# Reordered ScalarE, VectorE and TensorE work in a fused attention and expert layer, and a routing table made in six pieces instead of two

## The chip, the cores and the metric

The kernel runs on one core of one Trainium2 chip. The metric is the device time of one execution in microseconds (us). Five engines run side by side, each through its own instructions in program order, and wait for one another on semaphores: PE (TensorE, matrix products and transposes), ACT (ScalarE), DVE (VectorE), POOL (GpSimd) and SP (SyncE, which here only issues transfers).

## The reference, cut to what matters

2048 tokens of width 128 go through windowed attention (16 heads of 8, each query sees the 64 keys up to itself), a residual and a layer norm, and then through the two best of 8 experts, again with a residual and a layer norm.

```
x = layernorm(x + attn(x, w_qkv, w_out, b_out))
logits = x @ gate_w + gate_b;  topv, topi = top_k(logits, 2);  probs = softmax(topv)
for e in range(8):
    z = (x @ w1[e] + b1[e]) * (x @ w2[e] + b2[e])
    y = silu(z @ wg[e] + bg[e]) @ w3[e] + b3[e]
    out += (sum of probs where topi == e) * y
x = layernorm(x + out)
```

## The kernel before

**Attention in slots.** The tokens are 16 tiles of 128; two tiles form a unit of 256 whose queries, keys and values are projected together. Each engine has a function `slot(t, s)` that is called once per tile and lists, by hand, what that engine does in that slot for several tiles at different stages; a few slots are written out, slots 4 to 11 are a loop of four bodies. The order in which the calls stand in `slot` is the engine's order of work. A call with `later(t, -2)` works on the tile of two slots ago. Slots with an even number are even slots: they project keys and values; odd slots turn the tokens and project queries.

**One tile's way.** PE makes rough scores against slotted keys (`max_scores`, line 1349, from `k_slots` and `q_quarters`); DVE takes the row maxima (`find_top`, 949) and spreads them (`spread_top`, 959, tile `shift`); PE makes the exact scores less the maxima (`shifted_scores`, 1366 and 1370, from the stacked `q_stack` and `k_stack`), in two halves, a = 0 and a = 1; ACT takes exponentials (`exps`, 810); PE weighs the values (1385) into `o_bank`; ACT copies that bank out (`copy_values`, 821, tile `o_raw`); PE transposes it (`turn_values`, 1395); DVE takes reciprocals of the denominators and divides (`denominators` 973, `divide` 979); PE transposes again (`heads_T`, 1400), ACT copies (`oT`, 816), PE projects (1405). Then DVE and POOL normalise, and route: `x1_T` 1419, gate logits 1426, DVE logits 1017, ranks 1432, places 1043 to 1060, scatter to the DRAM table `routed` by POOL (664).

**A unit's way to the stacks.** In an even slot PE projects the keys of a unit used two slots later (1315). ACT copies their rounded part (788), DVE the rest (`split_keys`, 1008, tile `k_parts`). SP waits for it, stores both to DRAM (418), issues eight loads into `q_stack` (409) and four into `k_stack` (422), then four loads of expert weights. From the same rounded part ACT makes the four `key_slots` (795), needed by `max_scores` at the start of the next slot. In odd slots ACT copies the projected queries (774) and makes four `q_quarters` from them (779), needed only a slot after the next one's start.

**Expert stage.** The tokens are then worked on in 39 tiles of 128 routed rows, again in slots (`tile_slot`), with five stages of different tiles in one slot. Tiles 0 to 16 come from a table made on DVE after 12 of the 16 token tiles (`early_table`), the other 22 from a second table that DVE makes within the first tile slots. `run_end` calls a piece of remaining work after each of the first slots: `pieces` names them. Each step of a table is a `link`: one small DVE instruction, and a wait for its own completion. SP waits for the whole second table ahead of its load for tile 17 (in slot 14), PE and POOL ahead of tile 17.

## Time and profile before

| | |
|---|---|
| median of 3 runs | 317.65 us (317.65 to 318.34) |
| profiled execution: its time, and the span of its trace | 318.13 us, 316.3 us |
| attention, from `heads_T` of slot 4 to that of slot 12: 61.54 to 128.79 us | four units, 67.25 us |
| expert tiles | about 162 to 291 us |
| PE, DVE, ACT, POOL busy, share of the span | 76%, 69%, 48%, 50% |

The profile follows one execution. Busy time counts an engine's own instructions; a row of the timeline ends in square brackets where the engine stood idle ahead of it, with the instruction that released it. A row that ends in x4 stands for four instructions merged from the first start to the last end.

### The profile page before, as it was taken

To read this page: it belongs to the slowest core of one execution; us is meant where nothing else is said; L and a number is where in the kernel's file an instruction comes from. 1 tells how busy PE (TensorE), PEld (TensorE's weight loads), DVE (VectorE), ACT (ScalarE), POOL (GpSimd) and SP (SyncE) were. 2 spreads that over 40 slices of the span, in tenths; PEclk is the share of its full clock that TensorE was granted. 3 is DMA by queue.
4 is the path that set the end of the run, shared out by engine and by line. 5 is a ranking of instruction groups with operands and counts; after the bars stand their busy time and mean duration, and the time that the engine had idled before them with its cause. 6 is when DMAs were issued, how large, how long until landed. Compare 5 with 4: busy or idle time off the path is not lost.

```text
span 316.3 us, 7675 instructions
## 1 busy us (share of the span) xinstructions
PE 241.9 (76%) x1791; PEld 177.1 (56%) x1791; DVE 218.1 (69%) x714; ACT 153.3 (48%) x410; POOL 159.2 (50%) x287
## 2 busy tenths in 40 slices
PE   2485798787878788898588775999999999996000
PEld 1154576565667666687355554767677667664000
DVE  5499645778777878786747577687777777674091
ACT  3554636677666677755325542344443443442043
POOL 6654002556566656667763472333455455546151
PEclk9998959999999999999859999899999999999555
DMA  4662625249685968685521021311111111100522
GB/s 130 182 161 68 172 72 135 68 138 272 188 233 168 253 177 233 183 229 181 214 71 37 9 60 36 100 45 52 51 53 37 38 45 53 39 26 7 181 119 99
DMA packets 33988, 36.50 MB, mean 115 GB/s; under 512 B 4972, under 2 KB 30062, under 8 KB 33824
## 3 DMA queue, kind: packets, MB, share of 16 engines
q1 hardware_dynamic: 30864, 29.69, 32.8%
q0 software_dynamic: 2336, 4.37, 4.0%
q10 hardware_dynamic: 752, 2.03, 1.9%
q8 instruction: 14, 0.23, 0.3%
q14 instruction: 22, 0.18, 0.2%
HBM read 25.48 MB, written 11.05 MB: 115 GB/s over the span
## 4 chain that ended last, share of the span: by engine, by line
PE 60%; DVE 11%; ACT 11%; issue 9%; DMA 4%; DVEq 1%; POOL 1%; SPq 1%; ACTq 0%; POOLq 0%
PE bank L1551 10%; PE bank L1523 10%; PE bank L1514 6%; PE bank L1366 5%; PE bank L1370 4%; PE bank L1385 3%; PE bank L1349 3%; PE bank L1395 3%; ACT k_slots L795 3%; PE bank L1546 3%; ACT q_quarters L779 2%; PE bank L1539 2%; PE bank L1347 2%; ACT probs L810 2%; PE bank L1315 2%
## 5 line engine op out<-in xcount | busy, mean ns | idle before, releaser
L713 POOL DMA_INDIRECT expert_out<-probs,tile_x x39 | 40.4, 1035 | 57.7 <-DVE probs L1245 56.2
L810 ACT ACTIVATE probs<-bank 128x512 f32<-128x512 f32 x64 | 35.0, 595 | 39.7 <-PE bank L1370 39.7
L664 POOL DMA_INDIRECT routed<-rows,place x32 | 33.8, 1057 | 21.4 <-issue 16.5
L1523 PE MATMUL bank<-w_gate,x_all 128*128 x156 | 41.2, 388 | 0.4 <-DVE v_aug L1236 0.4
L1551 PE MATMUL bank<-w_up,x_unit 128*128 x78 | 41.4, 613 | 0.0
L949 DVE TENSOR_REDUCE top<-bank 128x4 f32<-128x384 f32 x64 | 33.5, 549 | 8.7 <-PE bank L1349 7.9
L1250 DVE TENSOR_TENSOR w_rows<-bank,b_up 128x512 f32<-128x512 f32 x39 | 26.9, 689 | 17.3 <-PE bank L1551 17.1
L1514 PEld LDWEIGHTS bank<-w_down,xT 128*128 128x128 f32 x156 | 20.8, 193 | 31.9 <-issue 31.9
L959 DVE TENSOR_TENSOR shift<-top,delta_block 64x256 fp32r<-64x256 f32 x64 | 31.0, 485 | 8.5 <-PE bank L1370 6.9
L883 ACT COPY x_unit<-bank 128x128 f32<-128x128 f32 x39 | 10.3, 265 | 53.8 <-PE bank L1531 53.8
L1514 PE MATMUL bank<-w_down,xT 128*128 x156 | 27.4, 299 | 8.2 <-DVE y_in L1231 5.8
L1366 PE MATMUL bank<-q_stack,k_stack 128*128 128x256 f32 x128 | 29.3, 311 | 1.2 <-issue 1.2
L1523 PEld LDWEIGHTS bank<-w_gate,x_all 128*128 128x128 f32 x156 | 27.2, 195 | 2.7 <-issue 0.4
L1370 PE MATMUL bank<-shift,shift_w 128*128 128x256 f32 x128 | 26.5, 290 | 0.0
L1349 PE MATMUL bank<-k_slots,q_quarters 128*128 128x384 f32 x64 | 25.9, 464 | 0.0
L1366 PEld LDWEIGHTS bank<-q_stack,k_stack 128*128 128x128 f32 x128 | 21.1, 202 | 1.6 <-issue 1.6
L1385 PE MATMUL bank<-probs,v_aug 128*32 128x128 f32 x512 | 21.9, 292 | 0.0
L1347 PE MATMUL bank<-mask_q,rep_b 128*128 128x256 bf16 x60 | 17.9, 299 | 4.6 <-ACT k_slots L795 2.1
L1254 DVE TENSOR_TENSOR x_all<-w_rows 128x256 f32<-128x256 f32 x39 | 19.8, 507 | 1.3
L898 ACT ACTIVATE v_aug<-v_aug 128x256 f32<-128x256 f32 x39 | 16.5, 422 | 8.7 <-DVE v_aug L1236 8.2
L1370 PEld LDWEIGHTS bank<-shift,shift_w 128*128 128x128 f32 x128 | 20.7, 198 | 0.0
L628 POOL TENSOR_SCALAR inv_std<-mean_var 128x1 f32<-128x1 f32 x16 | 4.6, 286 | 31.7 <-DVE mean_var L998 31.5
(177 smaller groups left out, 539.6 us busy)
## 6 DMA issues: line engine op xcount, KB each, us to landing
k_stack<-k_scratch SPq DMA_DIRECT2D x28, 160.0 KB, 3.2
q_stack<-q_scratch SPq DMA_DIRECT2D x62, 64.0 KB, 2.3
tile_x<-routed SPq DMA_DIRECT2D x39, 65.0 KB, 1.8
k_scratch<-k_parts SPq DMA_DIRECT2D x7, 320.0 KB, 2.4
q_scratch<-q_parts SPq DMA_DIRECT2D x8, 256.0 KB, 2.4
w_up<-in_L_ffn_w_dram SPq DMA_DIRECT2D x16, 128.0 KB
w_gate<-in_L_ffn_wg_dram SPq DMA_DIRECT2D x8, 256.0 KB
b_up<-in_L_ffn_b_dram SPq DMA_DIRECT2D x2, 1024.0 KB
```

What stands on the lines that cost most here:

```text
L664: eng.indirect_dma_start(routed, bass.IndirectOffsetOnAxis(ap=place[i][:, k:k + 1], axis=0), rows[i][:, k, :], None, bounds_check=SPARE + ...
L713: eng.indirect_dma_start(expert_out, bass.IndirectOffsetOnAxis(ap=tile_x[i][:, P:P + 1].bitcast(I32), axis=0), y[i][:, :], None, bounds_ch ...
L810: eng.activation(probs[t[1] % 2][a][:, 512 * h:512 * h + 512], t_bank[h][:, :], ACT.Exp).then_inc(probs_ready, 1)
L949: eng.tensor_reduce(top[a][:, 4 * h:4 * h + 4], s_bank[h][:, 0:4 * BLOCK_KEYS].rearrange("p (s k) -> p s k", s=4), AX_X, ALU.max).then_inc ...
L959: eng.tensor_tensor(shift[a][half][r, :, :].rearrange("p s (b q) -> p b s q", b=2), top[a][r, :].rearrange("p (b s) -> p b s", b=2).unsque ...
L1349: eng.matmul(scores, q_quarters[i][:, 2 * w + h, :, :].rearrange("p g q -> p (g q)"), k_slots[i][:, :, at:at + BLOCK_KEYS], start=False, s ...
L1366: eng.matmul(t_bank[h][:, 256 * l:256 * l + 256], k_stack[i][:, grp, QT * w:QT * w + P], q_stack[i][:, grp, :, QT * w:QT * w + QT], start= ...
L1370: ins = eng.matmul(t_bank[h][:, 256 * l:256 * l + 256], shift_w[:, h, l, first, :], shift[a][h][:, :, :], start=False, stop=(l == 1), skip ...
L1385: ins = eng.matmul(o_bank[32 * j:32 * j + 32, o:o + P], v_aug[i][:, w, j, 2 * HD * pair:2 * HD * pair + 32], probs[t[1] % 2][a][:, c:c + P])
L1514: ins = eng.matmul(down_bank[:, 0:P], actT[m[1] % 2][:, c, :], w_down[:, bass.ds(e[4], 1), c, :].rearrange("p o n -> p (o n)"), start=(c = ...
L1523: ins = eng.matmul(gate_bank[:, 0:F], zT[m[1] % 2][:, c, :], w_gate[:, bass.ds(e[2], 1), c, :].rearrange("p o n -> p (o n)"), start=(c == ...
L1551: eng.matmul(up_bank[:, :], tile_xT[n[1] % 2][:, :], of_expert(w_up, e[0])).then_inc(up_made, 1)
```

## The change: what it does

ACT, even slots: `key_slots` stands ahead of the second exponentials, and `copy_values` ahead of `values`. ACT, odd slots: `queries` is split, and `copy_values` goes between the copy of the queries and the four query blocks. PE: `turn_values` moves behind the first `shifted_scores`. DVE: the first `spread_top` moves ahead of `denominators` and `divide`. The second table's two pieces (after tile slots 6 and 7) become six (after slots 6 to 11); the 14 links are the same. SP pads the ends of the expert regions after slot 8, as before.

```diff
-            pieces = {0: "values", 1: "project", 2: "ranks", 3: "x1", 4: "logits", 5: "places", 6: "totals", 7: "table",
-                      8: "rows"}
+            pieces = {0: "values", 1: "project", 2: "ranks", 3: "x1", 4: "logits", 5: "places", 6: "totals", 7: "need",
+                      8: "ends", 9: "passed", 10: "jumps", 11: "table"}
...
                 eng.activation(q_parts[:, 0, :], unit_bank[:, 0:UNIT], ACT.Copy, scale=SCALE).then_inc(q_hi, 1)
+
+            def query_blocks(u):
+                i = u[1] % 2
                 wait(eng, q_hi, ucount(u, 1, 1))
...
-                if has(s, 0, STEPS - 1):
-                    exps(t, 1)
                 if s == -2:
...
-                if t[1] % 2 == 0 and has(s, 0, STEPS - 2):
-                    values(unit_at(t, 0))
+                if has(s, 0, STEPS - 1):
+                    exps(t, 1)
                 if odd:
                     queries(unit_at(t, 3))
                 if has(s, 1, STEPS):
                     copy_values(later(t, -1))
+                if odd:
+                    query_blocks(unit_at(t, 3))
+                if t[1] % 2 == 0 and has(s, 0, STEPS - 2):
+                    values(unit_at(t, 0))
...
+                if find:
+                    spread_top(top_t, 0, 0)
+                    spread_top(top_t, 0, 1)
                 if adds:
                     denominators(res_t)
                     divide(res_t)
-                if find:
-                    spread_top(top_t, 0, 0)
-                    spread_top(top_t, 0, 1)
...
                 elif name == "totals":
+                    rest_totals()
+                elif name == "need":
                     rest_needed()
+                elif name == "ends":
+                    rest_ends()
+                elif name == "passed":
+                    passed_of(REST, table_chain)
+                elif name == "jumps":
+                    jumps_of(REST, rest_row0[:, :], table_chain)
                 elif name == "table":
                     rest_table()
...
+                if has(s, 0, STEPS - 1):
+                    shifted_scores(t, 0)
                 if has(s, 2, STEPS + 1):
                     turn_values(later(t, -2))
-                if has(s, 0, STEPS - 1):
-                    shifted_scores(t, 0)
```

The new functions hold the old links: `rest_totals` the total and the two instructions of the padding rows, `rest_needed` three links, `rest_ends` three, `passed_of` two, `jumps_of` three, and `table_of`, called by `rest_table`, two.

ACT's order in even slot 12, before (`probs` are the exponentials, `k_parts` the rounded keys, `oT` the turned heads, `v_aug` the values, `o_raw` the weighted values):

```order
L810 ACTIVATE probs<-bank 128x512 x2
L827 COPY x1T<-bank 128x128
L788 CAST k_parts<-bank 128x320
L816 COPY oT<-bank 128x128
L810 ACTIVATE probs<-bank 128x512 x2
L795 ACTIVATE k_slots<-k_parts,slot_col 128x320 x4
L802 COPY v_aug<-bank 128x16x2x16
L821 COPY o_raw<-bank 128x2x4x64
L831 ACTIVATE gap<-gap 128x1
```

The same slot in the changed kernel, where lines from 774 on stand three further down:

```order
L813 ACTIVATE probs<-bank 128x512 x2
L830 COPY x1T<-bank 128x128
L791 CAST k_parts<-bank 128x320
L819 COPY oT<-bank 128x128
L798 ACTIVATE k_slots<-k_parts,slot_col 128x320 x4
L813 ACTIVATE probs<-bank 128x512 x2
L824 COPY o_raw<-bank 128x2x4x64
L805 COPY v_aug<-bank 128x16x2x16
L834 ACTIVATE gap<-gap 128x1
```

The key slots passed the second exponentials, and `o_raw` passed `v_aug`. The end of ACT's odd slot 3, before:

```order
L816 COPY oT<-bank 128x128
L810 ACTIVATE probs<-bank 128x512 x2
L774 ACTIVATE q_parts<-bank 128x256
L779 ACTIVATE q_quarters<-q_parts,quarter_col 128x8x32 x4
L821 COPY o_raw<-bank 128x2x4x64
L831 ACTIVATE gap<-gap 128x1
```

The same place in the changed kernel:

```order
L819 COPY oT<-bank 128x128
L813 ACTIVATE probs<-bank 128x512 x2
L774 ACTIVATE q_parts<-bank 128x256
L824 COPY o_raw<-bank 128x2x4x64
L782 ACTIVATE q_quarters<-q_parts,quarter_col 128x8x32 x4
L834 ACTIVATE gap<-gap 128x1
```

The copy of the weighted values now stands ahead of the four query blocks. DVE in even slot 12, before, from the second row maximum on (`shift` is the spread maxima, `o_den` and `o_norm` the reciprocals and the division, `logits` the gate's):

```order
L949 TENSOR_REDUCE top<-bank 128x4
L41 REGISTER_ALU
L973 RECIPROCAL o_den<-bank 128x16
L979 TENSOR_TENSOR o_norm<-bank,o_den 128x128
L959 TENSOR_TENSOR shift<-top,delta_block 64x2x4x32 x2
L1008 TENSOR_TENSOR k_parts<-bank,k_parts 128x320
L1017 TENSOR_TENSOR logits<-bank,gate_bias 128x8
```

And in the changed kernel:

```order
L954 TENSOR_REDUCE top<-bank 128x4
L964 TENSOR_TENSOR shift<-top,delta_block 64x2x4x32 x2
L41 REGISTER_ALU
L978 RECIPROCAL o_den<-bank 128x16
L984 TENSOR_TENSOR o_norm<-bank,o_den 128x128
L1013 TENSOR_TENSOR k_parts<-bank,k_parts 128x320
L1022 TENSOR_TENSOR logits<-bank,gate_bias 128x8
```

The two spreads no longer stand between the division and the logits; in odd slots, which split no keys, nothing stands there.

## Rows read from the trace of the kernel before

**Rows 1.** Busy by stretch: length, PE, PEld, DVE, ACT, POOL, clock, DMA share, GB/s

```profile
61.54:128.79 67.25, 55.15 (x604) 43.83 (x601) 52.16 (x200) 46.05 (x117) 42.13 (x89) 1.00 0.72 204
```

**Rows 2.** Timeline of PE: start us, us, operation, idle before and releaser

```profile
40.31 0.77 PE L1366 MATMUL bank<-q_stack,k_stack 128*128 128x256 f32 x2 [1.22 <-issue]
...
49.78 0.32 PE L1341 MATMUL bank<-mask_q,rep_b 128*128 128x384 bf16 x1 [1.08 <-issue]
...
58.81 0.63 PE L1395 MATMUL bank<-ident,o_raw 128*128 128x128 f32 x4 [1.68 <-ACT o_raw L821]
...
103.66 0.33 PE L1400 MATMUL bank<-ident,o_norm 128*128 128x128 f32 x1
...
109.43 0.63 PE L1395 MATMUL bank<-ident,o_raw 128*128 128x128 f32 x4 [1.80 <-ACT o_raw L821]
...
117.07 0.33 PE L1341 MATMUL bank<-mask_q,rep_b 128*128 128x384 bf16 x1 [1.08 <-ACT k_slots L795]
...
147.21 0.66 PE L1395 MATMUL bank<-ident,o_raw 128*128 128x128 f32 x4 [0.57 <-ACT o_raw L821]
```

**Rows 3.** Timeline of ACT, end of an odd slot and of the next even one

```profile
106.98 1.71 ACT L779 ACTIVATE q_quarters<-q_parts,quarter_col 128x256 fp32r<-128x256 f32 x4
108.59 0.56 ACT L821 COPY o_raw<-bank 128x512 f32<-128x512 f32 x1
...
113.96 1.09 ACT L810 ACTIVATE probs<-bank 128x512 f32<-128x512 f32 x2 [1.16 <-PE bank L1370]
114.93 1.91 ACT L795 ACTIVATE k_slots<-k_parts,slot_col 128x320 fp32r<-128x320 f32 x4
```

**Rows 4.** Timeline of DVE, an odd slot's logits to the next slot's key split

```profile
104.15 0.17 DVE L1017 TENSOR_TENSOR logits<-bank,gate_bias 128x8 f32<-128x8 f32 x1 [0.41 <-PE bank L1426]
...
107.35 0.42 DVE L1002 SCALAR_TENSOR_TENSOR q_parts<-bank,q_parts 128x256 fp32r<-128x256 f32 x1
...
108.39 1.02 DVE L949 TENSOR_REDUCE top<-bank 128x4 f32<-128x384 f32 x2
110.10 0.26 DVE L973 RECIPROCAL o_den<-bank 128x16 f32<-128x16 f32 x1 [0.69 <-PE bank L1395]
110.46 0.29 DVE L979 TENSOR_TENSOR o_norm<-bank,o_den 128x128 f32<-128x128 f32 x1
111.05 0.87 DVE L959 TENSOR_TENSOR shift<-top,delta_block 64x256 fp32r<-64x256 f32 x2 [0.30 <-PE bank L1370]
112.18 0.49 DVE L1008 TENSOR_TENSOR k_parts<-bank,k_parts 128x320 fp32r<-128x320 f32 x1 [0.26 <-ACT k_parts L788]
```

**Rows 5.** Timeline of SP's issues, the same unit's key stacks

```profile
118.50 1.97 SPq L422 DMA_DIRECT2D k_stack<-k_scratch  x4
```

**Rows 6.** The page's transfers: count, KB each, median us from issue to landing

```profile
k_stack<-k_scratch SPq DMA_DIRECT2D x28, 160.0 KB, 3.2
```

**Rows 7.** Timeline of DVE, tile slots 6 to 10: each begins with y_in

```profile
185.33 0.29 DVE L1231 TENSOR_TENSOR y_in<-bank,b_down 128x128 f32<-128x128 f32 x1 [0.65 <-issue]
...
190.32 0.29 DVE L1231 TENSOR_TENSOR y_in<-bank,b_down 128x128 f32<-128x128 f32 x1 [1.15 <-issue]
...
192.45 0.15 DVE L1122 SCALAR_TENSOR_TENSOR jump<-need,taken_step 1x8 f32<-1x8 f32 x1
...
194.48 0.17 DVE L1083 TENSOR_SCALAR tile_row<-probs 1x22 int32<-1x22 f32 x1
195.64 0.29 DVE L1231 TENSOR_TENSOR y_in<-bank,b_down 128x128 f32<-128x128 f32 x1 [0.99 <-DVE tile_row L1083]
...
198.41 0.29 DVE L1231 TENSOR_TENSOR y_in<-bank,b_down 128x128 f32<-128x128 f32 x1 [0.56 <-issue]
...
202.71 0.29 DVE L1231 TENSOR_TENSOR y_in<-bank,b_down 128x128 f32<-128x128 f32 x1 [0.59 <-issue]
```

**Rows 8.** Busy by stretch, columns as in group 1, 10 us of tile slots

```profile
190.00:200.00 10.00, 6.88 (x29) 5.37 (x30) 7.24 (x24) 2.25 (x8) 2.59 (x3) 0.83 0.21 61
```

More of the change, by code:

```diff
@@ L541, in piece @@
             def piece(name):
-                if name == "rows":
+                if name == "ends":
                     pad_ends()
@@ L1072, in ends_of, with passed_of @@
                 link(eng.tensor_reduce(ends[:, :], ends_2[:, :, :], AX_X, ALU.add), chain)
-            def tiles_of(first, n, row0, chain):
+            def passed_of(n, chain):
                 link(eng.tensor_tensor(passed[:, 0:n, :], ends[:, :].unsqueeze(1).to_broadcast([1, n, E]),
@@ L1078, in tiles_of, with jumps_of @@
                 link(eng.tensor_reduce(table_f[:, 0, 0:n], passed[:, 0:n, :], AX_X, ALU.add), chain)
+            def jumps_of(n, row0, chain):
                 link(eng.tensor_tensor(jumps[:, 0:n, :], passed[:, 0:n, :], jump[:, :].unsqueeze(1).to_broadcast([1, n, E]), ALU.mult), chain)
@@ L1081, in tiles_of, with table_of @@
                 link(eng.tensor_tensor(table_f[:, 1, 0:n], table_f[:, 1, 0:n], row0, ALU.add), chain)
+            def table_of(first, n, chain):
                 link(eng.tensor_scalar(tile_expert[:, 4 + first:4 + first + n], table_f[:, 0, 0:n], float(E - 1), None, ALU.min), chain)
@@ L1096, in early_table @@
                 link(eng.tensor_scalar(jump[:, :], need[:, :], -float(P), float(REGION), ALU.mult, ALU.add), early_chain)
-                tiles_of(0, FULL, tile_row0[:, 0:FULL], early_chain)
+                passed_of(FULL, early_chain)
+                jumps_of(FULL, tile_row0[:, 0:FULL], early_chain)
+                table_of(0, FULL, early_chain)
                 link(eng.tensor_scalar(taken_upto[:, 1:E + 1], ends[:, :], float(FULL), None, ALU.min), early_chain)
@@ L1104, in early_table, with rest_totals @@
                 assert links[0] == EARLY_LINKS
-            def rest_needed():
+            def rest_totals():
                 links[0] = 0
@@ L1113, in rest_needed @@
                 eng.tensor_copy(pad_row[:, :], pad_f[:, :]).then_inc(pad_chain, 1)
+            def rest_needed():
                 link(eng.tensor_tensor(need_16[:, :, :], total[:, :].unsqueeze(2).to_broadcast([1, E, 16]),
@@ L1117, in rest_needed, with rest_ends, rest_table @@
                 link(eng.tensor_tensor(need[:, :], need[:, :], taken[:, 0:E], ALU.subtract), table_chain)
+            def rest_ends():
                 ends_of(need, table_chain)
-            def rest_table():
                 link(eng.scalar_tensor_tensor(out=jump[:, :], in0=need[:, :], scalar=-float(P), in1=taken_step[:, :],
                                               op0=ALU.mult, op1=ALU.add), table_chain)
-                tiles_of(FULL, REST, rest_row0[:, :], table_chain)
+            def rest_table():
+                table_of(FULL, REST, table_chain)
                 assert links[0] == LATE_LINKS
```

## The prediction

> **What bounds the kernel now.** I read the busy time by stretch first, to see which stage is worth what, then the timelines of PE, ACT and DVE in the attention loop beside the chain of waits, then DVE's in the first expert slots. Over four units of attention PE is busy 55.15 of 67.25 us [rows 1]: a unit takes 16.81 us and PE works 13.79 of them, so 3.0 us are PE's idle time, at a granted clock of 1.00, which is 2.4 GHz. PE's timeline names the idle time [rows 2]: in an even slot it waits 1.80 us for the copy of the weighted values, and at the start of the next odd slot 1.08 us for the key slots. ACT's timeline says why [rows 3]. The copy ran at 108.59, behind 1.71 us of query blocks that no one needs before the next even slot; the key slots ran at 114.93, behind two exponentials of 1.09 us that PE needs only a slot later. The same two waits stand in all four units, so this stage is bound by the order of work on ACT, with PE close behind it.
>
> In the expert stage PE and DVE are about even. One slot is special: a tile slot without a piece runs from 195.64 to 198.41, that is 2.77 us, on DVE alone, while the two slots with a table piece take 4.99 (185.33 to 190.32) and 5.32 (to 195.64), and one more takes 4.30 (198.41 to 202.71) [rows 7], when the granted clock had fallen (0.83 on average, a mixture of 2.4 and 1.2 GHz) [rows 8].
>
> **ACT and PE, the units.** Both waits go if the copy comes 1.71 us earlier and the key slots 1.09 us earlier. With nothing in their place a unit would take PE's 13.8 us. I do not expect that, because two other loops are close.
>
> *DVE.* I walk DVE's order with rows [rows 4]. From an odd slot's logits at 104.15 to the next slot's first row maximum at 108.39 it takes 4.24 us without a pause, of which 0.42 is the query split that an even slot lacks: 3.82 there. Then come two maxima (1.02), the two spreads (0.87), the reciprocal with its gap (0.36) and the division (0.29), 2.5 us together. Before, the spreads stood behind the division, and worked while PE made the next thing that DVE needs. Now nothing does in an odd slot: DVE waits while PE transposes the divided heads and multiplies by the gate, 0.49 us from 103.66 [rows 2] to 104.15, and some 0.06 more for the semaphore (an estimate): a hole of 0.55. In an even slot the key split (0.49) fits in it. Odd: 4.24 + 2.5 + 0.55 = 7.3; even: 3.82 + 2.5 + 0.55 = 6.9; a unit 14.2, or 14.7 if ACT's rounding of the keys comes so late that the split follows the hole.
>
> *The stacks.* A unit's keys go through DRAM, and the loads must have landed when `shifted_scores` of the slot after the next begins. From the end of the key split (112.67) [rows 4] to the last issue, some 1.5 us into the four that start at 118.50 [rows 5], and 3.2 us to landing [rows 6], it is 10.5 us; nearly all of it is SP issuing one transfer after another. Before it, from the start of the turn at 109.43 to the split's end, 3.24 us hold one turn and the first `shifted_scores`; the new order swaps the two, so it is 3.24 us from the start of `shifted_scores`. 3.24 + 10.5 = 13.75 us, and 14.35 where the query blocks, now last in ACT's slot, push the first exponentials and the rounding of the keys back by some 0.6 (an estimate from the 1.71 us of rows 3, less what PE's maxima and first scores cover). So this loop, hidden today, becomes a bound as close as DVE.
>
> I take 14.6 us for a unit, near the upper ends, since both loops must be met in each slot. Four units: 67.25 - 58.4 = **8.85 us** won; bounds 13.8 (12.1 won) and 15.8 (4.0 won, below).
>
> *Second exponentials late.* They are now behind the key slots. In the trace they start 4.53 us after the turn (113.96 from 109.43) [rows 2, 3]; in the new order the key slots can start at about 3.24, end at 5.15, and the exponentials at 6.24. The next `shifted_scores` that needs their bank starts a slot later: 115.99, where PE ran out of work (117.07 less 1.08), plus two maxima of about 0.3 each, is 7.2 us after 109.43. The cover is 0.9 us; what goes beyond it is paid on PE. I take nothing. The values' copy behind the weighted values' is wanted only a slot later: nothing.
>
> **First units.** In slot 2 PE already waits for a stack, 1.22 us to 40.31 [rows 2]. There the turn was done in the waiting time; now it stands behind it, which costs its 0.63. The waits of 1.08 at 49.78 and 1.68 at 58.81 go [rows 2], and I take off one DVE hole of 0.55: 1.08 + 1.68 - 0.63 - 0.55 = **1.6 us** won; 1.0 to 2.1.
>
> **Last slots.** From slot 12 on there are no new units, DVE's slots lose the query split but have the hole, and the stacks of the last unit come as late as before: nothing. The wait of 0.57 at 147.21 [rows 2] goes, as `turn_values` now comes after 1 us of scores: **0.55 us** won.
>
> **The table.** DVE has no free time in these slots (2.77 us of its own), so its links cost full time wherever they stand; what six pieces can change is the ends. The second piece's links run from 192.45 to 194.65, 2.2 us, but its slot is 2.55 longer than 2.77 [rows 7]: 0.35 are lost as DVE waits for the last link before it reads the experts' numbers, where else that read runs beside the last product. Five of the six pieces end in such a wait, against two: 3 x 0.35 = 1.05 more. Against that, slots 9 and 10 cost 4.30 - 2.77 = 1.53 for the clock, which fell after PE had stood still for 2 us twice; with about 1 us six times I expect it to stay. Won: 1.53 - 1.05, about **0.5 us**, bounds -1 (the clock falls all the same) and +1.6.
>
> The Trainium skill, "VectorE: DVE Perf Modes", section "The DRAIN you can't avoid", states that a semaphore after each Vector instruction cost nothing against one after the last (13.88 us both ways). By that the cut would be free, and this part would give 1.5 instead of 0.5. The rows speak against it here, as what waits is the read behind the link, not a Vector instruction. No page is needed for the sum.
>
> **Sum.** 8.85 + 1.6 + 0.55 + 0.5 = 11.5 us. The profiled execution took 318.13 us (a span of 316.3 and 1.8 around it), which gives 306.6. It lay 0.5 above the median of 317.65, so the median would be 306.1; I take **306.5**, since each loop above has little air.
>
> **The rivals.**
> - *PE alone bounds* (13.8 us a unit): the holes of DVE fall where PE is busy anyway. For it: DVE was busy 52.16 us of 67.25 [rows 1], 13.0 a unit. Against it: its order is strict and the hole is a loop through PE. 67.25 - 55.2 = 12.1 in place of 8.85, and 0.5 more in the first units: 302.7.
> - *The stacks bound harder.* The same bytes come in less time: a DMA share of 0.72 [rows 1] becomes 0.72 x 16.81 / 14.6 = 0.83. If landing and issue stretch by 1.5 us, a unit takes 15.8, and 4.0 us are won in place of 8.85: 311.4. For it: in slot 2 the wait is there already. "DMA: Bandwidth & Descriptors" in the Trainium skill, section "Latency and other measured facts", gives HBM access as 0.2 us on average and 2 us at high load, which would do just this; no row here shows k_stack at a higher share.
> - *The cut is free* (each piece ends as cheaply as a product): 1 us less, 305.5. For it only that the ends of the two old pieces are two cases.
> - *Slower.* If the stacks are late in every unit, the turn, the division and all behind it, which used to run in that wait as in slot 2, now start after it, 0.63 each time. It decides from a landing of about 3.2 + 2.5 = 5.7 us on, where 14.35 becomes 16.85; at 6.5 a unit takes 17.6, and four cost 3.2 more than now: about 319.
> - *No effect*: the copies go earlier, and some other wait of the same size follows, 316 to 318.
>
> **How the numbers follow.** The forecast 0.45, PE alone 0.13, the free cut 0.10, the stacks harder 0.22, no effect 0.04, slower 0.06. About 0.3% (1 us) can be told from no change here. Faster then holds all but the last two, 0.90; same 0.04; slower 0.06. For 8 in 10 the range reaches to PE alone (302.7) below, and just beyond the stacks' case (311.4) above, which leaves out half of each with the last two: 302.0 to 312.0.
>
> **What would show it.** Right: in the profile after, PE's waits for `o_raw` in even slots and for `k_slots` in odd ones are gone, a unit takes 14 to 15 us, DVE is idle about half a microsecond ahead of its logits in odd slots, PE waits for the division at `heads_T`, and now and then at the first `shifted_scores` of an even slot for nothing that an engine released, as at 40.31. In the tile slots 6 to 11 each lasts 3.2 to 4.1 us, and none after them 4.3. Wrong: a unit of 15.5 us or more with PE waiting at 1366 (the stacks); waits at 1366 for exponentials (ACT's new order too late); a granted clock under 1.00 in the loop; or four tile slots from the first piece on that are together no shorter than the 17.4 us from 185.33 to 202.71.

## The result, and the profile after

The changed kernel takes 312.28 us (median of 4 runs, 311.62 to 313.58) against 318.0 us before (4 runs, 317.65 to 320.23): a ratio of 0.9848, 95% interval 0.9808 to 0.9888. That is 5.7 us faster where 11.5 were forecast, and just outside the range. The profiled execution took 311.95 us, with a span of 310.2 (316.3 before). The same kernel's times differ between chips and between runs by more than these first runs show (before: 310.68 to 323.55 in one set below), so each experiment stands against runs of before on its own chip, disturbed runs are left out of the ratios, and lengths read in the traces carry the argument.

First the busy time by stretch, columns as in [rows 1]: the same four units, then 50 us of tile slots.

```profile
59.66:121.43 61.77, 54.78 (x603) 43.87 (x601) 52.40 (x201) 46.69 (x117) 43.00 (x88) 1.00 0.77 220
160.00:210.00 50.00, 41.06 (x210) 27.80 (x208) 34.77 (x115) 20.70 (x58) 19.62 (x28) 1.00 0.16 46
```

Four units take 61.77 us in place of 67.25, so 15.44 each where 14.6 were forecast. PE's work is the same; its idle time is 7.0 us instead of 12.1. PE's timeline of the changed kernel says which waits these are:

```profile
40.61 0.76 PE L1393 MATMUL bank<-q_stack,k_stack 128*128 128x256 f32 x2 [5.47 <-issue]
...
56.81 0.38 PE L1393 MATMUL bank<-q_stack,k_stack 128*128 128x256 f32 x1 [1.19 <-DMA k_stack<-k_scratch]
...
67.05 0.33 PE L1427 MATMUL bank<-ident,o_norm 128*128 128x128 f32 x1 [0.54 <-DVE o_norm L984]
...
72.38 0.47 PE L1393 MATMUL bank<-q_stack,k_stack 128*128 128x256 f32 x2 [1.37 <-issue]
...
88.57 0.50 PE L1393 MATMUL bank<-q_stack,k_stack 128*128 128x256 f32 x2 [1.71 <-DMA k_stack<-k_scratch]
...
103.41 0.47 PE L1393 MATMUL bank<-q_stack,k_stack 128*128 128x256 f32 x2 [0.62 <-issue]
...
113.60 0.33 PE L1427 MATMUL bank<-ident,o_norm 128*128 128x128 f32 x1 [0.52 <-DVE o_norm L984]
...
121.43 0.33 PE L1427 MATMUL bank<-ident,o_norm 128*128 128x128 f32 x1 [0.77 <-DVE o_norm L984]
```

The two waits of [rows 2], for `o_raw` and for `k_slots`, are gone from the units. In their place stand a wait at the first `shifted_scores` (line 1393 now) of even slots, for the key stacks, and one of half a microsecond for the division in each odd slot (and 0.77 in the one even slot that waits for no stack). Both were named in the prediction as loops close behind. What it had wrong is how close.

**The stacks' chain.** SyncE's issues of one unit in the changed kernel:

```profile
76.33 0.42 SPq L418 DMA_DIRECT2D k_scratch<-k_parts  x1
77.05 5.18 SPq L409 DMA_DIRECT2D q_stack<-q_scratch  x8
82.28 1.97 SPq L422 DMA_DIRECT2D k_stack<-k_scratch  x4
...
92.30 0.38 SPq L418 DMA_DIRECT2D k_scratch<-k_parts  x1
```

I read three stretches, from one awaited `shifted_scores` to the next: to the keys' issue to DRAM, from there to the end of the last stack's issue, and from there to PE's start. From 56.81 on they are 3.58 + 8.62 + 3.37 = 15.57 us, from 72.38 on 3.95 + 7.92 + 4.32 = 16.19, from 88.57 on 3.73 + 7.82 + 3.29 = 14.84. The forecast, in the same parts, was 3.24 to 3.84, 7.80 (112.67 to 120.47) and 2.7. Where the trace has the landings, in the first and the third of these units, the last key stack landed at 72.29 and 103.32, and PE began 0.09 us later each time.

**VectorE's loop.** The unit from slot 10 to slot 12 had no wait for a stack; VectorE's timeline there:

```profile
106.77 0.17 DVE L1022 TENSOR_TENSOR logits<-bank,gate_bias 128x8 f32<-128x8 f32 x1
...
110.86 1.02 DVE L954 TENSOR_REDUCE top<-bank 128x4 f32<-128x384 f32 x2
...
113.26 0.29 DVE L984 TENSOR_TENSOR o_norm<-bank,o_den 128x128 f32<-128x128 f32 x1
114.09 0.17 DVE L1022 TENSOR_TENSOR logits<-bank,gate_bias 128x8 f32<-128x8 f32 x1 [0.55 <-PE bank L1453]
...
118.69 1.02 DVE L954 TENSOR_REDUCE top<-bank 128x4 f32<-128x384 f32 x2
...
121.92 0.17 DVE L1022 TENSOR_TENSOR logits<-bank,gate_bias 128x8 f32<-128x8 f32 x1 [0.15 <-PE bank L1453]
```

The hole of 0.55 us is there, as forecast. But from logits to logits it is 7.32 and 7.83 us, a unit of 15.15, not 14.2 to 14.7. The stretch to the next row maximum takes 4.09 and 4.60 (forecast 3.82 and 4.24), the rest 3.23 each time (3.05).

**Where the 6.1 us of the span came from.** `heads_T` of slot 4 is 1.88 us earlier (59.66 against 61.54), the units give 5.48, the last slots 0.45. Then 0.92 is lost up to the first tile slots (`y_in` of slot 6 at 178.44 against 185.33, 6.89 earlier), 0.42 in the slots with the table, and 0.37 after them. Two of these parts hold a share of PE's clock. From `heads_T` of slot 2 to that of slot 3, before and after:

```profile
44.37:53.13 8.76, 7.57 (x78) 6.17 (x74) 4.92 (x14) 5.38 (x14) 2.06 (x5) 0.90 0.53 151
```

```profile
44.70:51.63 6.93, 6.62 (x78) 5.59 (x74) 5.33 (x14) 5.88 (x14) 1.96 (x5) 1.00 0.43 118
```

Of the 1.83 us that this slot gives, 0.95 is PE's own work done at a higher granted clock. From the last `heads_T` but one to the last, beside the first tiles, it is the other way round, before and after:

```profile
158.45:167.05 8.60, 7.64 (x38) 4.62 (x39) 3.70 (x18) 2.18 (x8) 5.46 (x13) 0.59 0.30 72
```

```profile
150.64:160.15 9.51, 8.37 (x37) 4.98 (x38) 3.70 (x18) 2.33 (x8) 6.30 (x13) 0.52 0.42 116
```

Here 0.91 is lost, and PE's own work takes 0.73 longer, at a lower granted clock.

**The table.** VectorE's timeline, `y_in` of tile slots 6 to 12:

```profile
178.44 0.29 DVE L1258 TENSOR_TENSOR y_in<-bank,b_down 128x128 f32<-128x128 f32 x1 [0.64 <-issue]
181.94 0.29 DVE L1258 TENSOR_TENSOR y_in<-bank,b_down 128x128 f32<-128x128 f32 x1 [0.84 <-issue]
185.91 0.29 DVE L1258 TENSOR_TENSOR y_in<-bank,b_down 128x128 f32<-128x128 f32 x1 [1.05 <-issue]
189.67 0.29 DVE L1258 TENSOR_TENSOR y_in<-bank,b_down 128x128 f32<-128x128 f32 x1 [0.99 <-DVE jump L1138]
193.48 0.29 DVE L1258 TENSOR_TENSOR y_in<-bank,b_down 128x128 f32<-128x128 f32 x1 [0.99 <-DVE probs L1083]
197.49 0.29 DVE L1258 TENSOR_TENSOR y_in<-bank,b_down 128x128 f32<-128x128 f32 x1 [0.99 <-DVE probs L1089]
202.06 0.29 DVE L1258 TENSOR_TENSOR y_in<-bank,b_down 128x128 f32<-128x128 f32 x1 [0.99 <-DVE tile_row L1094]
```

and SyncE's issues beside them, with the wait on PE:

```profile
189.61 5.37 SPq L515 DMA_DIRECT2D routed<-pad  x8
195.75 1.48 SPq L530 DMA_DIRECT2D tile_x<-routed  x2
```

```profile
197.86 0.33 PE L1558 MATMUL bank<-ident,tile_x 128*128 128x128 f32 x1 [2.24 <-DMA tile_x<-routed]
```

The clock stays at 1.00 from 160 to 210 us, as forecast (0.83 before, [rows 8]). But all six pieces end in a wait of 0.84 to 1.05 us, where the two slots without a piece in [rows 7] have 0.56 and 0.59. And ahead of slot 11's work a tile's load stands behind eight pads, 5.4 us of SyncE, and PE waits 2.24 us for it. Slots 6 to 12 take 26.38 us in place of 25.96.

### The profile page after: what moved, and what is told of

Same layout as the page of the kernel before. It is cut to its first block, busy times and chain, and to the rows that moved or that the text cites. A ratio compares the mean times of both kernels' runs of the same rounds, so it can differ in the third digit from the quotient of the medians.

```text
span 310.2 us, 7675 instructions
## 1 busy us (share of the span) xinstructions
PE 237.9 (77%) x1791; PEld 174.1 (56%) x1791; DVE 217.2 (70%) x714; ACT 154.1 (50%) x410; POOL 161.0 (52%) x287
## 4 chain that ended last, share of the span: by engine, by line
PE 47%; DVE 14%; SPq 12%; issue 12%; DMA 8%; POOL 3%; ACT 2%; DVEq 0%; ACTq 0%; POOLq 0%
PE bank L1578 9%; PE bank L1550 8%; PE bank L1541 6%; SPq L409 5%; PE bank L1393 3%; DMA k_stack<-k_scratch 3%; PE bank L1573 2%; PE bank L1397 2%; PE bank L1566 2%; PE bank L1412 2%; DMA expert_out<-probs,tile_x 2%; DVE top L954 2%; SPq L422 2%; DVE shift L964 2%; DMA w_up<-expert_out 2%
## 5 line engine op out<-in xcount | busy, mean ns | idle before, releaser
L1550 PE MATMUL bank<-w_gate,x_all 128*128 x156 | 40.4, 382 | 0.5 <-DVE v_aug L1263 0.5
L1277 DVE TENSOR_TENSOR w_rows<-bank,b_up 128x512 f32<-128x512 f32 x39 | 26.8, 688 | 18.5 <-PE bank L1578 18.3
L964 DVE TENSOR_TENSOR shift<-top,delta_block 64x256 fp32r<-64x256 f32 x64 | 30.1, 471 | 11.9 <-PE bank L1397 9.5
L1393 PE MATMUL bank<-q_stack,k_stack 128*128 128x256 f32 x128 | 28.4, 305 | 10.9 <-issue 7.4
L1376 PE MATMUL bank<-k_slots,q_quarters 128*128 128x384 f32 x64 | 25.0, 449 | 0.0
L1412 PE MATMUL bank<-probs,v_aug 128*32 128x128 f32 x512 | 21.1, 283 | 0.0
L628 POOL TENSOR_SCALAR inv_std<-mean_var 128x1 f32<-128x1 f32 x16 | 5.4, 338 | 27.9 <-DVE mean_var L1003 27.2
```

The lines of the kernel that those rows point to most:

```text
L964: eng.tensor_tensor(shift[a][half][r, :, :].rearrange("p s (b q) -> p b s q", b=2), top[a][r, :].rearrange("p (b s) -> p b s", b=2).unsque ...
L1277: eng.tensor_tensor(up[:, :, :].rearrange("p a n -> p (a n)"), up_bank[:, :], of_expert(b_up, e[0]), ALU.add).then_inc(up_ready, 1)
L1393: eng.matmul(t_bank[h][:, 256 * l:256 * l + 256], k_stack[i][:, grp, QT * w:QT * w + P], q_stack[i][:, grp, :, QT * w:QT * w + QT], start= ...
L1412: ins = eng.matmul(o_bank[32 * j:32 * j + 32, o:o + P], v_aug[i][:, w, j, 2 * HD * pair:2 * HD * pair + 32], probs[t[1] % 2][a][:, c:c + P])
L1550: ins = eng.matmul(gate_bank[:, 0:F], zT[m[1] % 2][:, c, :], w_gate[:, bass.ds(e[2], 1), c, :].rearrange("p o n -> p (o n)"), start=(c == ...
```

## The experiments

Lengths of units are from `heads_T` to `heads_T` of even slots. A unit is called clean where PE waits for no stack in it.

**First set: parts undone.** e1_paired loads the expert weights for two experts at a time:

```
-                if s is None:
+                if s is None and t[1] % 2 == 0:
-                        eng.dma_start(w_up[:, bass.ds(e, 1), c, :], ...
+                        eng.dma_start(w_up[:, bass.ds(e, 2), c, :], ...
```

> The changed kernel with the expert weights of two experts in one transfer, issued in the even slots alone: the same bytes, but 4 weight issues a unit on SyncE in place of 8. A unit takes 15.44 us in the changed kernel. Issue theory (SyncE's time to issue transfers one after the other, some 0.5 us each, fills the loop of the stacks): the stacks' last issue comes about 2 us earlier in the unit, PE's waits of 0.6 to 1.7 us at the first shifted_scores of even slots go, a unit takes 14.5 to 14.7, the time is 308 to 309 us. Traffic theory (the same bytes in less time make each transfer land later): the bytes are the same, so the unit stays at 15.3 to 15.5 and the time at 311.5 to 312.5. VectorE theory (its order with the spreads ahead of the division is the bound): the waits at shifted_scores go, but PE waits as long elsewhere, for o_norm or sparse: unit 15.2 or more, time above 311.

Measured: 313.27 us in its profiled execution, 313.27 to 321.62 in four runs, with before at 310.68 to 323.55 beside it, so the time says nothing. PE's waits for the stacks are 1.0 to 3.1 us: longer, not gone. SyncE's issues show that the edit did something else as well:

```profile
100.94 0.38 SPq L458 DMA_DIRECT2D q_scratch<-q_parts  x1
105.05 0.37 SPq L418 DMA_DIRECT2D k_scratch<-k_parts  x1
107.08 1.20 SPq L409 DMA_DIRECT2D q_stack<-q_scratch  x2
```

The queries' transfer to DRAM now stands behind four weight transfers of twice the size, and the query stacks, which wait for it, begin 6.1 us after it and 2.0 behind the keys (0.7 in the changed kernel). So this run doesn't tell the theories apart.

e2_old_dve puts the spreads back behind the division, e3_two_pieces the table back into two pieces, e4_act_only both, and the turn back ahead of the scores:

```
-                if find:
-                    spread_top(top_t, 0, 0)
-                    spread_top(top_t, 0, 1)
                 if adds:
                     denominators(res_t)
                     divide(res_t)
+                if find:
+                    spread_top(top_t, 0, 0)
+                    spread_top(top_t, 0, 1)
```

> The changed kernel with the two spreads behind the division again, as before. VectorE theory (the hole of 0.55 us that this left in each slot bounds the loop): a unit gets up to 1 us shorter, 14.4 to 14.9, and PE's waits of 0.5 us for o_norm in odd slots go: 308 to 310 us. Issue and traffic theories: the waits for o_norm go, the waits for the stacks get longer by as much, unit 15.3 to 15.6, 311.5 to 312.5 us.

> The changed kernel with the second table in two pieces as before, and the pads issued after the second of them; the attention part is untouched. Table slots 6 to 13 take 26.4 us in the changed kernel against 26.0 before. Theory that six ends cost more than they give: 25.5 to 26.0, 311 to 312 us, so 0.4 to 0.9 less than the changed kernel, with the granted clock falling again behind the second piece. Theory of the prediction (two pieces cost 0.5 more through the clock): 312.5 to 313.

> Only the part on ScalarE (key slots ahead of the second exponentials, copies of values ahead of the query blocks); values turned ahead of the scores, spreads behind the division, and the table in two pieces as before. Issue and traffic theories: PE's two waits of 1.80 and 1.08 us go here too, and the stacks bound the unit as in the changed kernel, or come earlier by one turn (0.63 us) less: unit 15.0 to 15.9, 311 to 314 us. If the other edits of the loop carry the gain (the turn behind the scores above all): unit 16 or more, 314.5 us or more. If VectorE's and PE's edits cost time: unit 14.6 to 15.0, 308 to 310 us.

Measured: e2 314.54 us in its profiled execution, with PE's waits for `o_norm` down to one of 0.15 in the units, and waits of 1.4 to 2.7 us for the stacks in three of them; the fourth is clean and takes 14.41. e3: ratio 1.012 (0.994 to 1.030), so the time tells nothing; its table slots take 26.08 us and the clock falls behind the second piece (0.76 over slot 9). Three of its units are clean: two take 14.88 and 15.13, and one 15.76, with a wait of 1.14 us for the division. e4: 0.992 (0.982 to 1.002), 309.11 us when profiled, and its clean unit takes 14.09. By time this set can't place ScalarE's part alone against the whole change. What it shows is that undoing VectorE's part alone mostly turned its wait into a longer one for the stacks (62.73 us for e2's four units against 61.77), and that a unit without such a wait is then shorter (14.41 against 15.15).

**Second set: the same start for all.** In the traces of before and after, VectorE stands still early on. In the changed kernel it is the spread at 23.55:

```profile
23.55 4.13 DVE L964 TENSOR_TENSOR shift<-top,delta_block 64x256 fp32r<-64x256 f32 x2 [0.69 <-PE bank L1397]
27.71 0.49 DVE L1013 TENSOR_TENSOR k_parts<-bank,k_parts 128x320 fp32r<-128x320 f32 x1
```

and on GpSimd at that time:

```profile
22.38 4.57 POOL L677 TENSOR_TENSOR x_all<-x_all,bo 128x2048 f32<-128x2048 f32 x1
```

Two spreads, 0.87 us elsewhere, take 4.13: the first ends at 27.23, 0.28 us behind the end of GpSimd's add at 26.95 (27.44 and 27.16 in the trace of before). Behind them stands the key split, and the second unit's stacks are late by it. The Trainium skill, "SBUF — State Buffer", section "SBUF: two separate sides", says that a VectorE instruction with two SBUF inputs and a GpSimd one that reads SBUF take a shared pair of ports in turns, whole instructions at a time; the trace agrees (4.57 us for the add, 4.13 for the spreads). Four kernels let the add wait for that split; the first is the kernel before, the second, third and fourth are the whole change, ScalarE's part, and ScalarE's part with the stacks in two halves:

```
                 if s == 1:
                     eng.wait_ge(loaded, 16 * 4)
+                    eng.wait_ge(k_lo, 2)
```

```
-                    if s != -2:
-                        wait(eng, k_hi, ucount(u, 1, 1))
-                        wait(eng, k_lo, ucount(u, 1, 1))
-                        store_keys(eng, i).then_inc(k_out, 16)
...
                     for part in range(8):
+                        if s != -2 and part == 4:
+                            wait(eng, k_hi, ucount(u, 1, 1))
+                            wait(eng, k_lo, ucount(u, 1, 1))
+                            store_keys(eng, i).then_inc(k_out, 16)
```

> The kernel before, with one wait more: GpSimd's add of the bias to all tokens (4.56 us, at 22.60 in the trace of before) waits for the second key split on VectorE. In the trace of before two spreads on VectorE, 0.87 us elsewhere, took 5.11 us from 22.78, until that add was over, and the key split, and with it the second unit's stacks, came behind them, at 27.92. In the first of the runs above, where the split stood 0.2 us ahead of the add, it ran at 23.51. Theory that this one add holds VectorE: the split is at about 23.8, PE's wait at slot 2 ends some 4 us earlier, 313.5 to 314.5 us. Rival, the add holds a later instruction as long and the stacks are as late: 317 to 318.

> The changed kernel with that same wait on GpSimd; with the run of before with the wait it shows what the change is worth when the start is the same in both. Theory that the start is apart from the loop: 307.5 to 309 us, 5.5 to 6.5 less than before with the wait; units of 15.0 to 15.6 us. Rival, the gain of the start is lost in the loop to later stacks: 311 or more.

> ScalarE's part of the change alone, with the same wait on GpSimd. Theory that PE's and VectorE's moves cost time (the hole of 0.55 us ahead of the logits in each slot, and the turn that no longer fills the wait for the stacks): units without a wait for the stacks take 14.1 us, as the last of them did in the run of ScalarE's part alone, with it 15.0 to 15.6; 303.5 to 305.5 us, some 3 less than the whole change with the wait. Rival, that those moves are worth nothing either way: within 1 us of the whole change with the wait.

> As the kernel above, with four of the eight query stacks issued ahead of the keys' transfer to DRAM instead of behind it. Chain theory (what is late is the time from the key split through SyncE's issues to the landing): from the keys' issue to the end of the last stack's issue it is 5.2 to 5.8 us instead of 7.6, PE's waits at the first shifted_scores of even slots fall by about 2 us, most to nothing; a unit takes 14.0 to 14.5 us, 301 to 303 us. SyncE theory (the queue is full whatever its order, 14.4 us of issues a unit): waits of 0.3 to 0.8 stay, unit 14.5 to 14.8. Traffic theory (stacks land later under load): waits stay near 1 us, unit 15 or more, 304 to 305 us.

Measured, before being 316.96 us on that chip: e7 312.69 (ratio 0.989, 0.978 to 1.000), e8 306.21 (0.968, 0.958 to 0.978), e9 307.58 (0.965, 0.948 to 0.982), e10 303.14 (0.958, 0.947 to 0.968). The start is worth 4.3 us without the change by the medians, with an interval that reaches 1.000; in e7's trace `heads_T` of slot 4 stands at 55.42 in place of 61.54, and the four units take 67.17 as before. The add then holds a later spread as long (26.21 to 30.17 in e7), but no stack hangs on that one. From the same start the change is worth 6.5 us (2.1%, where the first comparison gave 1.5). e9 against e8 is open by time (302.73 to 309.38); its four units take 61.93 us against 63.55, with a wait for a late stack in every one. e10's time from the keys' issue to the end of the last stack's issue is down to 5.05 us, and two of its units still wait for stacks, 1.28 and 1.59 us.

**Third set: the weights out of the loop.** What delays the stacks: the weights' traffic, or the chain itself? In e11 (the whole change), e12 (ScalarE's part) and e13 (the whole change with the spreads put back), all with the later add and each run once, the loop loads no weights; the last four slots do:

```
-                if s is None:
-                    e = t[0] * 4 + (t[1] - 4)
...
+                    to, w = ((w_up[:, :, 0, :], w1), ...)[s - STEPS + 4]
+                    eng.dma_start(to ..., w ...).then_inc(experts_loaded, 16)
```

> The changed kernel with the later add on GpSimd, and with the expert weights (5 MB, 8 issues a unit) taken out of the loop: they are loaded whole, in one transfer a slot, in the last four slots behind the biases. The end of the kernel then waits for them and its time says nothing; what counts are the units from slot 4 to slot 12. Traffic theory (the stacks land 3.3 to 4.3 us behind their last issue because the weights share the way): landing back under 3 us, PE's waits for the stacks gone, and the unit at what VectorE's order leaves, 14.8 to 15.2 us, as in the units without such a wait so far. Chain theory (SyncE's 7.8 us of issues from keys to last stack): waits of 0.5 us or more stay, unit 14.8 to 15.4 with them.

> ScalarE's part alone, with the later add and with the weights out of the loop in the same way. Traffic theory: no waits for the stacks, and the unit at 14.0 to 14.2 us, all of it PE's work: 0.8 to 1.0 us a unit less than the whole change in the run above, which is then what PE's and VectorE's moves cost. Rival, those moves cost nothing: the same unit in both, within 0.2 us.

> The changed kernel with the later add and the weights out of the loop, and the spreads behind the division again: only the turn behind the scores is left of PE's and VectorE's moves. If the hole that the moved spreads left is the bound: PE's waits for o_norm go and the unit is 14.0 to 14.3 us, as with ScalarE's part alone. If the later turn is what costs: 14.7 or more, with PE waiting for something behind the turn.

Busy by stretch of e11's four units, columns as above, and the two waits on its PE:

```profile
56.25:117.77 61.52, 55.05 (x604) 43.91 (x602) 52.27 (x201) 46.70 (x117) 42.85 (x88) 1.00 0.50 140
```

```profile
69.14 0.36 PE L1389 MATMUL bank<-q_stack,k_stack 128*128 128x256 f32 x1 [1.55 <-issue]
...
84.53 0.50 PE L1389 MATMUL bank<-q_stack,k_stack 128*128 128x256 f32 x2 [0.92 <-DMA k_stack<-k_scratch]
```

```profile
72.48 0.36 SPq L418 DMA_DIRECT2D k_scratch<-k_parts  x1
73.14 5.07 SPq L409 DMA_DIRECT2D q_stack<-q_scratch  x8
78.25 1.97 SPq L422 DMA_DIRECT2D k_stack<-k_scratch  x4
```

The DMA share falls from 0.77 to 0.50, and the four units take 61.52 us instead of 61.77. From the end of the last stack's issue (80.22) to PE's start it is 4.31 us, as in the changed kernel (4.32), and in the unit before, to 69.14, 3.39 against 3.37. So the traffic theory falls, as far as it means the weights of this loop, and with it the reason that the prediction's rival gave. Eight fewer issues a unit change the chain little too: 3.34 + 7.74 + 4.31 = 15.39. e11's clean units take 14.87 and 15.16 us, e12's 14.42 and 14.36, and e13 waits 0.8 to 2.5 us for a stack in all four units. VectorE's and PE's moves together cost 0.5 to 0.8 us a clean unit, and without VectorE's the stacks bind.

> ScalarE's part alone with the later add, four query stacks ahead of the keys, and the expert weights two experts at a time, so that SyncE issues 4 transfers less in each unit. The run without the pairing still waited for the stacks in two units, where SyncE had got round to the keys late. If SyncE's full queue was the reason: at most one such wait, units of 14.0 to 14.6, 300 to 302 us. If landing under load is: the same waits, 302 to 304 us.

e14 took 313.81 us (ratio 0.979, 0.965 to 0.993), slower than e10 against its own before, with waits of 2.5 to 3.1 us for the stacks in three of its four units. Its query stacks wait for a transfer behind doubled weights as in e1. Its trace has the landing: the queries' transfer, issued at 98.11, landed at 104.68, and the query stacks' issues began at 104.70; in the kernel before such a transfer lands 2.4 us after its issue (median). So the pairing lengthened the loop in both orders that were tried.

**Fourth set: each loop shortened.** e15 is e8 with the stacks in two halves, e16 the same with the spreads behind the division, e17 with the turn ahead of the scores too, e18 is e8 again.

> The changed kernel with the later add and four of the eight query stacks issued ahead of the keys; PE's and VectorE's moves stay. If the chain of the stacks and VectorE's order are two loops of nearly the same length: PE's waits at the first shifted_scores go in most units, the waits of 0.5 us for o_norm stay in every slot, the unit is 14.9 to 15.2 us, and the time is some 1 to 2 us under the changed kernel with the later add in the last of these runs. If the stacks alone bound it: 14.1 to 14.5, 3 us or more.

> As the run above, and the spreads behind the division again; the turn stays behind the scores. Two-loops theory: both limits are away, unit 14.1 to 14.6 where no stack is late, 301 to 304 us. If the later turn costs as much as the hole did: 14.8 or more, no faster than the run above.

> As the run above, and the turn ahead of the scores again: ScalarE's part, the table in six pieces, the later add and the stacks in two halves. Against the same with the table in two pieces (303.14 us, in another set of runs) it shows whether the six pieces are worth anything: 0.5 us more or less at most by the table slots so far, so 302 to 304 us. Late stacks still to be seen in one or two units.

> The changed kernel with the later add once more, as what the three runs above stand against: 305 to 308 us, waits of 0.5 to 2 us for the stacks in two or three of the four units.

Measured, before being 319.81 us there: e15 305.25 (ratio 0.954, 0.946 to 0.963), e16 305.65 (0.949, 0.940 to 0.958), e17 305.35 (0.957, 0.948 to 0.966), e18 308.0 (0.963, 0.956 to 0.970). Two clean units of e15, and 4 us around its one late stack:

```profile
85.25:115.62 30.37, 27.89 (x305) 22.27 (x302) 25.79 (x101) 23.00 (x58) 20.00 (x43) 0.98 0.80 216
...
81.00:85.00 4.00, 3.67 (x31) 2.65 (x31) 2.13 (x6) 1.78 (x4) 2.00 (x4) 0.72 0.91 274
```

the waits in e15's PE timeline,

```profile
81.33 0.38 PE L1394 MATMUL bank<-q_stack,k_stack 128*128 128x256 f32 x1 [2.01 <-DMA k_stack<-k_scratch]
...
107.79 0.33 PE L1428 MATMUL bank<-ident,o_norm 128*128 128x128 f32 x1 [0.53 <-DVE o_norm L985]
```

and two units of e16 (the second with one wait of 0.50 us for a stack), with the same `heads_T` row without its wait:

```profile
85.05:113.53 28.48, 27.45 (x304) 21.94 (x300) 25.21 (x100) 23.24 (x58) 18.92 (x43) 1.00 0.83 222
```

```profile
106.25 0.33 PE L1428 MATMUL bank<-ident,o_norm 128*128 128x128 f32 x1
```

15.19 us a unit with the spreads moved, 14.24 with them put back, the turn being in its new place in both: the hole costs 0.95 us a unit once the stacks are out of the way, and the later turn at most 0.2 (14.20 for e16's first clean unit here, 14.01 and 14.02 for those of e10 and e19, where the turn is ahead). e15 and e16 still differ in nothing by time, as late stacks here and there outweigh it (waits of 1.9 to 2.8 us; behind the one above PE runs at a granted clock of 0.72). e15's 2.75 us against e18 came mostly ahead of slot 4, whose `heads_T` is 2.81 earlier. e17 against e10 (0.957 and 0.958 of before) shows no worth in the six pieces; its table slots take 27.01 us, e10's 25.81.

**Last set.**

> ScalarE's part alone, with the table in two pieces, GpSimd's later add and four query stacks ahead of the keys, beside the whole change on the same chip. By the two-loops theory and the start: 302 to 305 us, 6 to 10 less than the whole change and 13 to 15 less than before.

> The whole change once more, on the chip of the run above: 311 to 314 us; PE's wait for the stacks at slot 2 ends at about 40.5 us if GpSimd's add holds VectorE there again, and at 36 to 37 if it doesn't.

e19, which is e10 again, took 303.8 us (303.29 to 305.0; ratio 0.959, 0.954 to 0.965), the whole change on that chip 310.5 (306.75 to 313.71; 0.978, 0.969 to 0.987), before 318.31. e20 is the change without an edit, and its start went the other way:

```profile
23.41 0.87 DVE L964 TENSOR_TENSOR shift<-top,delta_block 64x256 fp32r<-64x256 f32 x2 [1.03 <-PE bank L1397]
24.41 0.49 DVE L1013 TENSOR_TENSOR k_parts<-bank,k_parts 128x320 fp32r<-128x320 f32 x1
24.82 1.01 DVE L954 TENSOR_REDUCE top<-bank 128x4 f32<-128x384 f32 x2
25.93 3.57 DVE L964 TENSOR_TENSOR shift<-top,delta_block 64x256 fp32r<-64x256 f32 x2
```

```profile
24.18 4.60 POOL L677 TENSOR_TENSOR x_all<-x_all,bo 128x2048 f32<-128x2048 f32 x1
```

```profile
36.02 0.47 PE L1393 MATMUL bank<-q_stack,k_stack 128*128 128x256 f32 x2 [2.28 <-issue]
```

GpSimd's add began 1.8 us later than in the first trace; by then the spreads were all but done, the split was not held, and PE's wait at slot 2 ended at 36.02 instead of 40.61; this execution took 308.87 us. So the same kernel has two starts, 4.6 us apart at slot 2, and which one it gets is decided by a race of VectorE with GpSimd. Not all of it reached the end: e20's four units take 63.61 us in place of 61.77, with a wait of 2.19 us for a stack in the first.

## Why the prediction was wrong

The mechanism was right, and sizes of its terms were off, the units' above all. Step by step:

**The waits removed.** Right: PE's waits for `o_raw` and `k_slots` are gone from all four units. Right too that the second exponentials, though later, cost nothing there: none of the waits that PE's timeline shows in the four units is put down to them.

**"I take 14.6 us for a unit, near the upper ends."** This is the step that failed: the term "units" is 5.48 us, not 8.85. Both loops that were meant to bound the unit were taken too short. VectorE's is 14.9 to 15.2 us in clean units of the change, e3, e8, e11, e15 and e20 (with one of 15.76 in e3 and one of 16.12 in e20, where PE waits 1.14 and 1.28 us for the division; why there is open), not 14.2 to 14.7: I walked it on the trace of before, with pieces of an order that no longer holds, and its two slots came out 0.4 and 0.5 us longer. The stacks' chain is 14.84 to 16.19, not 13.75 to 14.35. To the keys it is 3.58 to 3.95 us, the upper end of the forecast or 0.1 beyond it; the issues take up to 0.8 more; and the landing, the largest part, 0.6 to 1.6 more: I took the page's median of one transfer (3.2 us from its issue), but PE waits for the last of twelve, and began 3.3 to 4.3 us after the end of the last issue, where my sum had 2.7. With VectorE's 15.15 alone, the four units would have given 6.65; late stacks took the other 1.2.

**The rival "the stacks bound harder"** came nearest in its number (15.8 us a unit, 311.4), and its reason was wrong: with the DMA share at 0.50 in place of 0.77 the stacks were as late (e11). Of the higher latency at high load that the Trainium skill gives ("DMA: Bandwidth & Descriptors", section "Latency and other measured facts"), and that I weighed for it, no run here shows anything.

**First units, 1.6.** 1.88 came, close by luck: 0.95 of it is the higher granted clock between slots 2 and 3, which the sum did not have, and a wait of 1.19 us for a stack at 56.81, which it did not have either, stands against it. The wait at slot 2 is 5.47 us (1.22 before) and ends at 40.61 as before at 40.31: what the change won ahead of it was lost there, since that stack hangs on GpSimd's add, which the prediction had not seen.

**Last slots, 0.55.** 0.45, but as a net. The wait at 147.21 went, and so did one of 0.94 at 133.57, where the rough scores begin, which I had not counted; waits of 0.78 and 0.80 for the division (128.73 and 135.71) took it back.

**The table, +0.5.** -0.42. The clock stayed up, worth the 1.53 that were forecast (for slot 9; slot 10 took 2.76 before and lost nothing), but the pieces cost 2.0 us more and not 1.05, of which some 0.7 is slot 11 (4.57 us, from 197.49, against 3.5 to 4.0 for the others), where PE waited for a load behind the pads. Two pieces measure 25.6 to 26.8 us over these slots in eight traces, six pieces 26.1 to 27.7 in nine. The reading that the cut is free is refuted.

**Not forecast:** 0.9 us from the last attention slots to the first tiles. Some 0.3 is the first tile's load: PE takes up that tile 7.51 us earlier than before, and its step ahead 7.82. The other 0.6 comes right behind it, with PE's granted clock, 0.52 from the last `heads_T` but one to the last in place of 0.59: two products of an early tile took 1.05 us from 166.15 on before, and take 1.47 from 158.85 on now.

Left open is why the last stack takes 3.3 us in one unit and 4.3 in the next; it does so in the same units without the weights (e11). The best version, ScalarE's part with two pieces, the later add and the keys ahead of half of the query stacks, is 4% under before (e10, e19) and some 6 us (0.959 and 0.978 of before) under the whole change on the same chip.

## What to carry to other kernels

When a change removes the bound of a loop, walk every other loop in the order that the change makes, wait by wait, and take the last transfer of a group and not the median one. Where two loops come out within half a microsecond of each other, expect the longer one, and on top of it what the other adds when it is late (15.15 us a unit and 1.2 over four units here). If undoing one of two equal bounds changes nothing, that doesn't clear it: shorten the other first, and look again (e2 against e16). Read the lengths of clean units as well as the total, which here hid a start that went one way or the other.

## What the hardware showed that I had not expected

A GpSimd add of 128x2048 made VectorE's spreads 2.7 to 4.2 us longer (0.87 us for two elsewhere; 4.13 in the changed kernel, 5.11 in before, 3.57 in e20); the first of them ended 0.28 us behind the add in each of these three. It did not hold the row maximum ahead of them, which reads a bank: 1.01 us at 24.82 in e20, while the add ran. Halving what the DMA engines move in the loop (220 to 140 GB/s) left the landing of the stacks as it was, while with doubled weight transfers ahead of it on SyncE's queue a transfer of 256 KB landed only 6.6 us after its issue (e14; in e1 those that wait for it began 6.1 us after it), where the median of such transfers before is 2.4. And PE's clock fell after a wait of 2.01 us for a late stack (0.72 over the next 4 us, a mixture of 2.4 and 1.2 GHz, in e15), while after one of 1.71 (88.57 in the changed kernel) it stayed at 1.00. The length of the wait alone doesn't tell which: after one of 1.59 in e10 the clock was 0.57 over the next 4 us.
